# The last combination of a two-layer attention and mixture-of-experts kernel: eight buffer pairs, all loads at once, stores from ScalarE

## The chip, the cores and the metric

The kernel runs on one core of one Trainium2 chip. The metric is the device time of one execution in microseconds (us), as the median of several executions. Times inside the kernel come from the trace of one profiled execution and are counted from its first instruction.

## What is computed

The input `x` holds 8 sequences of 512 tokens with 128 features, float32. Four layers follow each other, each with a layer norm ahead of it and its result added to `x`:

```python
x = x + attn_a(layernorm(x), w_q, w_k, w_v1, w_v2)     # one head
x = x + ffn(layernorm(x), Wg, W1, W2, W3)              # 8 experts, each token goes to its best 2
x = x + attn_b(layernorm(x), Q, K, V, W)               # 16 heads
x = x + ffn(layernorm(x), Wg, W1, W2, W3)
return x
# in ffn:
topk_scores, topk_idx = top_k(xt @ Wg.T, 2)
y = einsum('teh,edh->ted', silu(xt @ W1) * (xt @ W2), W3)
out = sum over the token's two experts of topk_score * y[token, expert]
```

The change concerns the last line of the second `ffn`: for each token two rows of expert results are added to each other and to `x`, and the sum is the output.

## The kernel before

The kernel is a sequence of blocks: `prepare`, `attention_a`, `experts` ("f1"), `attention_b`, `experts` ("f2"). At the end of each block all engines meet: each one first drains itself, then signals, and nobody goes on before all have. These drains and signals are recorded with the line of the block's opening, L1032 for `experts`.

Within `experts`, 71 tiles of 128 rows (NT), already sorted by expert, pass through TensorE, ScalarE and VectorE. GpSimd (POOL) scatters each finished tile of results to the DRAM array `y_rows` with an indirect DMA (L1224): choice 0 of token n goes to row n, choice 1 to row 4096 + n. SyncE (SP) loads the tiles, and then waits until every scatter has landed (L1084).

Only in "f2" (`out` is not None) the final combination follows, sequence by sequence, b = 0 to 7 (NB), 256 KB per array and sequence:

- SP loads the two arrays of a sequence from `y_rows` into `yc[b % 2][0]` and `yc[b % 2][1]` (L1090). There are two such pairs, so that the load of sequence b waits until the additions of sequence b - 2 are done.
- POOL adds the pair (L1230).
- VectorE (DVE) adds the sum to the tokens in `x_tok` (L1214) and counts up `added`.
- SP stores the tokens of sequence b - 1 to the output (L1093, the last one L1096), in its program order behind the loads of sequence b and ahead of those of sequence b + 1, and waits at the end for all eight stores.

Both loads and stores move rows of 128 float32, 512 bytes each.

In "f1" there is no combination; it is done at the start of `attention_b`, which the change doesn't touch.

Of the kernel before, what the change touches and what calls it, by code (L numbers as in the profile page):

```python
# [4 lines left out]
F32 = mybir.dt.float32  # L5
F32R = mybir.dt.float32r
BF16 = mybir.dt.bfloat16
ALU = mybir.AluOpType
# [3 lines left out]
P = 128  # L12
NB, T, D = 8, 512, 128
QT = T // P
# [10 lines left out]
NK = 2  # L25
# [29 lines left out]
def wait(eng, sem, value):  # L55

    if not isinstance(value, int) or value > 0:
        eng.wait_ge(sem, value)
# [969 lines left out]
def experts(nc, g, name, pl, out=None):  # L1028
# [3 lines left out]
    with ExitStack() as ctx:  # L1032
        sb = lambda n, s, d: ctx.enter_context(nc.sbuf_tensor(f"{name}_{n}", s, d))
        pb = lambda n: ctx.enter_context(nc.psum_tensor(f"{name}_{n}", [P, 512], F32))
        sem = lambda n: ctx.enter_context(nc.semaphore(f"{name}_{n}"))
# [10 lines left out]
        y_sb = [sb(f"y_sb{i}", [P, D], F32) for i in range(NY)]  # L1046
        dest = sb("dest", [P, NT], I32)
        if out is not None:
            yc = [[sb(f"yc{i}_{k}", [P, QT, D], F32) for k in range(NK)] for i in range(2)]
        cleared = sem("cleared")  # L1050
        xs_in = [sem(f"xs_in{i}") for i in range(NX)]
        xs_turned = sem("xs_turned")
# [11 lines left out]
        y_done = sem("y_done")  # L1064
        y_out = [sem(f"y_out{i}") for i in range(NY)]
        if out is not None:
            yc_in = [sem(f"yc_in{i}") for i in range(2)]
            yc_summed = sem("yc_summed")
            added = sem("added")
            stored = sem("stored")  # L1070
        block = ctx.enter_context(nc.Block())

        @block.sync
        def _(sp):
            sp.wait_ge(pl.table_done, 2)
            for i in range(2):
                sp.wait_ge(pl.scattered[i], NB // 2 * NK * QT * 16)
            for i in range(NT):
                row = sp.value_load(pl.table[0:1, 1, i:i + 1], min_val=0, max_val=NE * CAP - P)
                wait(sp, hidden_done, i - NX + 1)  # L1080
                wait(sp, dest_done, i - NX + 1)
                sp.dma_start(xs[i % NX][:], g.x_sorted[bass.ds(row, P), :]).then_inc(xs_in[i % NX], 16)
            for i in range(NY):
                sp.wait_ge(y_out[i], len(range(i, NT, NY)) * 16)  # L1084
            if out is not None:
                for b in range(NB):
                    wait(sp, added, b - 1)
                    for k in range(NK):
                        rows = g.y_rows[k * CAP + b * T:k * CAP + b * T + T, :].rearrange("(t p) d -> p t d", p=P)
                        sp.dma_start(yc[b % 2][k][:], rows).then_inc(yc_in[b % 2], 16)  # L1090
                    if b > 0:
                        sp.wait_ge(added, b)
                        sp.dma_start(out[(b - 1) * T:b * T, :].rearrange("(t p) d -> p t d", p=P),  # L1093
                                     g.x_tok[:, (b - 1) * QT:b * QT, :]).then_inc(stored, 16)
                sp.wait_ge(added, NB)
                sp.dma_start(out[(NB - 1) * T:NB * T, :].rearrange("(t p) d -> p t d", p=P),  # L1096
                             g.x_tok[:, (NB - 1) * QT:NB * QT, :]).then_inc(stored, 16)
                sp.wait_ge(stored, NB * 16)

        @block.tensor  # L1100
# [60 lines left out]
        @block.scalar  # L1161
        def _(act):
            for s in range(NT + 2):
                if s < NT:
                    act.wait_ge(xs_turned, s + 1)
                    wait(act, up_full, s - 2)
                    nc.scalar.activation(xs_parts[s % 3][0][:], turn_bank[:, 0:P], ACT.Copy).then_inc(xs_hi_done, 1)
                i = s - 1
                if 0 <= i < NT:
                    act.wait_ge(gate_full, i + 1)  # L1170
                    wait(act, hidden_done, i - 1)
                    nc.scalar.activation(act_gate[i % 2][:], gate_bank[i % 2][:, 0:EH], ACT.Silu).then_inc(silu_done, 1)
                i = s - 2
                if 0 <= i < NT:
                    act.wait_ge(hid_turned, i + 1)
                    wait(act, y_full, i - 2)
                    nc.scalar.activation(hid_parts[i % 3][0][:], hid_bank[i % 2][:, 0:HW], ACT.Copy).then_inc(hid_hi_done, 1)  # L1177

        @block.vector
        def _(dve):  # L1180
            dve.wait_ge(pl.table_done, 2)
            dve.wait_ge(cleared, 4)
            for s in range(NT + 4):
                if s < NT:
                    dve.wait_ge(xs_in[s % NX], s // NX * 16 + 16)
                    nc.vector.copy_predicated(dest[:, s:s + 1], pl.valid[:, s:s + 1],
                                              xs[s % NX][:, DEST:DEST + 1].bitcast(I32)).then_inc(dest_done, 1)
                    dve.wait_ge(xs_hi_done, s + 1)
                    hi, lo = xs_parts[s % 3]
                    nc.vector.tensor_tensor(lo[:], turn_bank[:, 0:P], hi[:].bitcast(F32), ALU.subtract).then_inc(xs_lo_done, 1)  # L1190
                i = s - 1
                if 0 <= i < NT:
                    dve.wait_ge(up_full, i + 1)
                    dve.wait_ge(silu_done, i + 1)
                    wait(dve, hid_turned, i - 2)
                    nc.vector.scalar_tensor_tensor(hidden[i % 3][:, 0:EH], act_gate[i % 2][:], xs[i % NX][:, GATE:GATE + 1],
                                                   up_bank[i % 2][:, 0:EH], ALU.mult, ALU.mult).then_inc(hidden_done, 1)
                i = s - 4
                if 0 <= i < NT:
                    dve.wait_ge(y_full, i + 1)  # L1200
                    wait(dve, y_out[i % NY], i // NY * 16)
                    nc.vector.tensor_reduce(y_sb[i % NY][:], y_bank[:, 0:2 * P].rearrange("p (i d) -> p d i", i=2), AX.X,  # L1202
                                            ALU.add).then_inc(y_done, 1)
                i = s - 2
                if 0 <= i < NT:
                    dve.wait_ge(hid_hi_done, i + 1)
                    hi, lo = hid_parts[i % 3]
                    nc.vector.tensor_tensor(lo[:], hid_bank[i % 2][:, 0:HW], hi[:].bitcast(F32),  # L1208
                                            ALU.subtract).then_inc(hid_lo_done, 1)
            if out is not None:  # L1210
                for b in range(NB):
                    rows = g.x_tok[:, b * QT:b * QT + QT, :]
                    dve.wait_ge(yc_summed, b + 1)
                    nc.vector.tensor_tensor(rows, rows, yc[b % 2][0][:], ALU.add).then_inc(added, 1)  # L1214

        @block.gpsimd
        def _(pool):
            nc.gpsimd.memset(dest[:], NOWHERE).then_inc(cleared, 1)
            for h in hidden:
                nc.gpsimd.memset(h[:, EH:HW], 0.0).then_inc(cleared, 1)  # L1220
            for i in range(NT):
                pool.wait_ge(y_done, i + 1)
                pool.wait_ge(dest_done, i + 1)
                nc.gpsimd.indirect_dma_start(out=g.y_rows, out_offset=bass.IndirectOffsetOnAxis(dest[:, i:i + 1], 0),  # L1224
                                             in_=y_sb[i % NY][:], in_offset=None, bounds_check=NK * CAP - 1,
                                             oob_is_err=False).then_inc(y_out[i % NY], 16)
            if out is not None:
                for b in range(NB):
                    pool.wait_ge(yc_in[b % 2], (b // 2 + 1) * NK * 16)
                    nc.gpsimd.tensor_tensor(yc[b % 2][0][:], yc[b % 2][0][:], yc[b % 2][1][:],  # L1230
                                            ALU.add).then_inc(yc_summed, 1)


def attention_b(nc, g, pl):
# [370 lines left out]
def build(nc, ins, out):  # L1605
    g = Shared()
    g.spent = []
    with ExitStack() as ctx:
# [27 lines left out]
        with ExitStack() as half:  # L1636
            pl = Plan(nc, half, "f1_p")
            with ExitStack() as first:
                sb1 = lambda n, s: first.enter_context(nc.sbuf_tensor(n, s, F32R))
                pair1 = lambda n, s: (sb1(f"{n}_hi", s), sb1(f"{n}_lo", s))  # L1640
                g.xn_hi, g.xn_lo = pair1("xn", [P, NB * T])
                g.a_wq, g.a_wk = pair1("a_wq", [P, P]), pair1("a_wk", [P, P])
                g.a_wv1, g.a_wv2 = pair1("a_wv1", [P, KD]), pair1("a_wv2", [P, D])
                prepare(nc, g, ins)
                attention_a(nc, g, pl)
            experts(nc, g, "f1", pl)
        with ExitStack() as half:
            pl = Plan(nc, half, "f2_p")
            attention_b(nc, g, pl)
            experts(nc, g, "f2", pl, out)  # L1650
# [22 lines left out]
```

## Time and profile before

| | |
|---|---|
| median of three executions | 1532.55 us (1528.47 to 1534.16) |
| the profiled execution: time | 1528.65 us |
| its span, first to last instruction | 1526.9 us |
| part of the span from the first load of the combination | 1493.1 to 1526.9 us |
| POOL's last addition | 1519.6 to 1520.8 us |
| last store: issued, landed | 1521.6, 1523.9 us |
| last barrier signals | 1526.9 us |

The profile's page gives the span, the busy time of each engine, the share of each DMA engine's time that its packets took, and the chain of work that ended last. Views of the trace show single instructions in order of time, sums over a window, and the instructions of one line. "SPq" and "POOLq" are the instruction queues of the two engines; an entry there is an instruction that isn't counted as busy, such as a DMA issue or a drain.

### The profile page before, as it was taken

The numbers are of one execution on the slowest core, as the hardware profiler recorded it, in microseconds if no ns is written. First come the engines' busy times: TensorE is split into PE (matmuls) and PEld (weight loads), VectorE is DVE, ScalarE is ACT, GpSimd is POOL, SyncE is SP. The second block draws the span as 40 slices with busy tenths as digits, with TensorE's granted clock in tenths as the row PEclk, the third lists the DMA queues.
The fourth block names the chain that finished last, engine by engine and source line by source line (L and its number), as shares of the span: only waits on it lengthen the run. The fifth ranks groups of instructions, "written<-read, shape, count | busy, mean of one in ns | idle before, by whom it ended". The sixth has DMA issues, their size and how long they took to land. (4 is left out here: it accounts for less than half of the span.)

```text
span 1526.9 us, 28432 instructions
## 1 busy us (share of the span) xinstructions
PE 1309.5 (86%) x8377; PEld 1119.5 (73%) x8377; DVE 1098.0 (72%) x2822; ACT 941.9 (62%) x2522; POOL 765.3 (50%) x954
## 2 busy tenths in 40 slices
PE   1688635999679999999999999999999996399990
PEld 1576634999558888888888888888888885299980
DVE  5666544777548788888887888888888875277771
ACT  1554422444248888788788888787887884244440
POOL 3005563444335555575675665765765655244443
PEclk9986657999879999999999999999999997599995
DMA  9391011222100000000000000000000000122215
GB/s 180 115 378 37 29 38 50 62 61 60 38 28 1 2 15 1 1 25 5 5 25 1 20 10 1 22 8 2 11 5 5 10 3 11 34 62 59 60 45 165
DMA packets 91936, 64.47 MB, mean 42 GB/s; under 512 B 34020, under 2 KB 77935, under 8 KB 91792
## 3 DMA queue, kind: packets, MB, share of 16 engines
q1 hardware_dynamic: 83152, 45.75, 11.0%
q0 software_dynamic: 8640, 16.93, 3.5%
q8 instruction: 74, 1.21, 0.3%
q14 instruction: 70, 0.57, 0.1%
HBM read 26.59 MB, written 36.96 MB: 42 GB/s over the span
## 5 line engine op out<-in xcount | busy, mean ns | idle before, releaser
L1364 POOL TENSOR_TENSOR b_probs<-b_probs,b_recip 128x128 f32<-128x128 f32 (+3 forms) x512 | 352.7, 719 | 308.7 <-DVE b_recip L1597 308.7
L420 DVE TENSOR_TENSOR b_pt_lo<-b_ring,b_pt_hi 128x512 fp32r<-128x512 f32 (+1 forms) x384 | 219.0, 598 | 95.5 <-ACT b_pt_hi L414 90.1
L545 ACT ACTIVATE b_probs<-b_s_bank,b_neg_max 128x256 f32<-128x256 f32 (+3 forms) x512 | 267.9, 533 | 27.6 <-DVE b_neg_max L537 26.2
L537 DVE TENSOR_REDUCE b_neg_max<-b_s_bank 128x1 f32<-128x256 f32 (+3 forms) x512 | 219.7, 479 | 47.3 <-PE b_s_bank L529 46.3
L1224 POOL DMA_INDIRECT y_rows<-f_y_sb,f_dest x142 | 139.1, 979 | 193.4 <-DVE f_y_sb L1202 184.5
L414 ACT ACTIVATE b_pt_hi<-b_ring 128x512 fp32r<-128x512 f32 (+1 forms) x384 | 192.2, 547 | 11.4 <-PE b_ring L485 10.6
L485 PE MATMUL b_ring<-ident,b_probs 128*128 128x128 f32 x1280 | 179.1, 277 | 4.7 <-DVE b_q_lo L420 4.7
L81 PE MATMUL b_s_bank<-b_k_hi,b_q_hi 64*128 64x256 f32 (+3 forms) x512 | 180.6, 353 | 2.9 <-ACT b_probs L545 1.4
L1177 ACT ACTIVATE f_hid_hi<-f_hid_bank 128x384 fp32r<-128x384 f32 x142 | 69.9, 492 | 160.8 <-PE f_hid_bank L1130 143.7
L554 PE MATMUL b_pv_bank<-b_pt_hi,b_v 128*128 128x512 f32 (+3 forms) x512 | 160.0, 324 | 6.3 <-DVE b_y L1560 5.2
L82 PE MATMUL b_s_bank<-b_k_lo,b_q_hi 64*128 64x256 f32 (+3 forms) x512 | 164.4, 321 | 0.0
L83 PE MATMUL b_s_bank<-b_k_hi,b_q_lo 64*128 64x256 f32 (+3 forms) x512 | 163.8, 320 | 0.0
L485 PEld LDWEIGHTS b_ring<-ident,b_probs 128*128 128x128 f32 x1280 | 140.8, 141 | 21.6 <-DVE b_q_lo L420 10.8
L554 PE MATMUL b_pv_bank<-b_pt_lo,b_v 128*128 128x512 f32 (+3 forms) x512 | 148.1, 326 | 0.0
L1208 DVE TENSOR_TENSOR f_hid_lo<-f_hid_bank,f_hid_hi 128x384 fp32r<-128x384 f32 x142 | 79.2, 558 | 61.8 <-ACT f_hid_hi L1177 61.7
L1142 PE MATMUL f_y_bank<-w,f_hid_hi 128*128 x426 | 116.4, 342 | 3.5 <-DVE f_y_sb L1202 2.9
L81 PEld LDWEIGHTS b_s_bank<-b_k_hi,b_q_hi 64*128 64x128 f32 x512 | 95.2, 186 | 30.1 <-issue 15.0
L554 PEld LDWEIGHTS b_pv_bank<-b_pt_hi,b_v 128*128 128x128 f32 x512 | 97.7, 191 | 17.5 <-DVE b_pt_lo L420 6.2
L545 ACT ACTIVATION_READ_ACCUMULATOR b_probs<-b_s_bank,b_neg_max 128x1 f32 x512 | 108.4, 212 | 0.0
L554 PEld LDWEIGHTS b_pv_bank<-b_pt_lo,b_v 128*128 128x128 f32 x512 | 98.0, 191 | 8.4
L83 PEld LDWEIGHTS b_s_bank<-b_k_hi,b_q_lo 64*128 64x128 f32 x512 | 95.5, 187 | 6.1
L1142 PEld LDWEIGHTS f_y_bank<-w,f_hid_hi 128*128 128x128 f32 x426 | 79.9, 188 | 25.9 <-issue 21.9
(303 smaller groups left out, 3360.7 us busy)
## 6 DMA issues: line engine op xcount, KB each, us to landing
x_sorted<-a_blank SPq DMA_DIRECT2D x64, 260.0 KB, 3.8
f_xs<-x_sorted SPq DMA_DIRECT2D x142, 65.0 KB
b_yc<-y_rows SPq DMA_DIRECT2D x16, 256.0 KB, 3.1
f_yc<-y_rows SPq DMA_DIRECT2D x16, 256.0 KB, 3.3
y_rows<-f_y_sb,f_dest POOLq DMA_INDIRECT x142
x_tok<-in_L_attn_a_x_dram SPq DMA_DIRECT2D x8, 256.0 KB, 5.2
out_dram<-x_tok SPq DMA_DIRECT2D x8, 256.0 KB, 2.5
f_raw<-in_L_ffn_W_dram SPq DMA_DIRECT2D x1, 1408.0 KB, 6.4
```

The lines of the kernel that those rows point to most:

```text
L81: nc.tensor.matmul(out, st[0], mv[0], start=start, stop=False)
L82: nc.tensor.matmul(out, st[0], mv[1], start=False, stop=False)
L83: return nc.tensor.matmul(out, st[1], mv[0], start=False, stop=stop)
L414: nc.scalar.activation(dst, src(rg.of(key)), ACT.Copy).then_inc(rg.hi_done, 1)
L420: nc.vector.tensor_tensor(dst, src(rg.of(key)), hi.bitcast(F32), ALU.subtract).then_inc(rg.lo_done, 1)
L485: last = nc.tensor.transpose(rg.of(keys[k])[:, to:to + P], probs[:, P_AT[i] + j * P:P_AT[i] + j * P + P], ident[:])
L537: nc.vector.tensor_reduce(sc.neg_max[:, i:i + 1], s_tile(sc, i), AX.X, ALU.max, negate=True).then_inc(sc.max_done, 1)
L545: nc.scalar.activation(probs[:, P_AT[i]:P_AT[i] + (i + 1) * P], s_tile(sc, i), ACT.Exp, bias=sc.neg_max[:, i:i + 1], accum_out=sums[:, i:i ...
L554: last = nc.tensor.matmul(pv_bank[:, j * P:T], v_at(j), pt[part][:, PT_AT[j]:PT_AT[j] + T - j * P], start=(j == 0 and part == 0), stop=(j ...
L1142: nc.tensor.matmul(y_bank[:, 0:2 * P], hi[:, c * P:c * P + P], w3[:, bass.ds(at, 2 * P)], start=c == 0, stop=False)
L1224: nc.gpsimd.indirect_dma_start(out=g.y_rows, out_offset=bass.IndirectOffsetOnAxis(dest[:, i:i + 1], 0), in_=y_sb[i % NY][:], in_offset=Non ...
L1364: nc.gpsimd.tensor_tensor(part, part, recip[:, i:i + 1].to_broadcast([P, (i + 1) * P]), ALU.mult).then_inc(probs_done, 1)
```

## The change

Each of the eight sequences gets its own pair of buffers and its own semaphore. SP issues all sixteen loads with no wait between them. The stores are issued by ScalarE (ACT), each after `added` has reached its sequence. POOL does the first addition for even sequences only; for odd ones VectorE does it, counts `summing` up, waits for it and does the second addition.

```diff
         if out is not None:
-            yc = [[sb(f"yc{i}_{k}", [P, QT, D], F32) for k in range(NK)] for i in range(2)]
+            yc = [[sb(f"yc{b}_{k}", [P, QT, D], F32) for k in range(NK)] for b in range(NB)]
...
-            yc_in = [sem(f"yc_in{i}") for i in range(2)]
+            yc_in = [sem(f"yc_in{b}") for b in range(NB)]
             yc_summed = sem("yc_summed")
+            summing = sem("summing")
...
                 for b in range(NB):
-                    wait(sp, added, b - 1)
                     for k in range(NK):
                         rows = g.y_rows[k * CAP + b * T:k * CAP + b * T + T, :].rearrange("(t p) d -> p t d", p=P)
-                        sp.dma_start(yc[b % 2][k][:], rows).then_inc(yc_in[b % 2], 16)
-                    if b > 0:
-                        sp.wait_ge(added, b)
-                        sp.dma_start(out[(b - 1) * T:b * T, :].rearrange("(t p) d -> p t d", p=P),
-                                     g.x_tok[:, (b - 1) * QT:b * QT, :]).then_inc(stored, 16)
-                sp.wait_ge(added, NB)
-                sp.dma_start(out[(NB - 1) * T:NB * T, :].rearrange("(t p) d -> p t d", p=P),
-                             g.x_tok[:, (NB - 1) * QT:NB * QT, :]).then_inc(stored, 16)
+                        sp.dma_start(yc[b][k][:], rows).then_inc(yc_in[b], 16)
                 sp.wait_ge(stored, NB * 16)
...
         # ScalarE, after its last tile
+            if out is not None:
+                for b in range(NB):
+                    act.wait_ge(added, b + 1)
+                    act.dma_start(out[b * T:b * T + T, :].rearrange("(t p) d -> p t d", p=P),
+                                  g.x_tok[:, b * QT:b * QT + QT, :]).then_inc(stored, 16)
...
         # VectorE, after its last tile
                     rows = g.x_tok[:, b * QT:b * QT + QT, :]
-                    dve.wait_ge(yc_summed, b + 1)
-                    nc.vector.tensor_tensor(rows, rows, yc[b % 2][0][:], ALU.add).then_inc(added, 1)
+                    if b % 2:
+                        dve.wait_ge(yc_in[b], NK * 16)
+                        nc.vector.tensor_tensor(yc[b][0][:], yc[b][0][:], yc[b][1][:], ALU.add).then_inc(summing, 1)
+                        dve.wait_ge(summing, b // 2 + 1)
+                    else:
+                        dve.wait_ge(yc_summed, b // 2 + 1)
+                    nc.vector.tensor_tensor(rows, rows, yc[b][0][:], ALU.add).then_inc(added, 1)
...
         # GpSimd, after its last scatter
-                for b in range(NB):
-                    pool.wait_ge(yc_in[b % 2], (b // 2 + 1) * NK * 16)
-                    nc.gpsimd.tensor_tensor(yc[b % 2][0][:], yc[b % 2][0][:], yc[b % 2][1][:],
-                                            ALU.add).then_inc(yc_summed, 1)
+                for b in range(0, NB, 2):
+                    pool.wait_ge(yc_in[b], NK * 16)
+                    nc.gpsimd.tensor_tensor(yc[b][0][:], yc[b][0][:], yc[b][1][:], ALU.add).then_inc(yc_summed, 1)
```

## Rows read from the trace of the kernel before

**Rows 1.** Timeline, window 1484 to 1527: start us, duration us, engine, line, operation, [idle before <- releaser]

```profile
1490.87 0.98 POOL L1224 DMA_INDIRECT y_rows<-f_y_sb,f_dest  x1 [0.63 <-issue]
1493.12 2.03 SPq L1090 DMA_DIRECT2D f_yc<-y_rows  x4
1496.69 1.26 POOL L1230 TENSOR_TENSOR f_yc<-f_yc,f_yc 128x512 f32<-128x512 f32 x1 [4.85 <-DMA f_yc<-y_rows]
1497.98 0.69 DVE L1214 TENSOR_TENSOR x_tok<-x_tok,f_yc 128x512 f32<-128x512 f32 x1 [7.89 <-POOL f_yc L1230]
1498.68 1.26 POOL L1230 TENSOR_TENSOR f_yc<-f_yc,f_yc 128x512 f32<-128x512 f32 x1 [0.73 <-DMA f_yc<-y_rows]
1498.70 0.38 SPq L1093 DMA_DIRECT2D out_dram<-x_tok  x1
1499.13 1.09 SPq L1090 DMA_DIRECT2D f_yc<-y_rows  x2
1499.97 0.69 DVE L1214 TENSOR_TENSOR x_tok<-x_tok,f_yc 128x512 f32<-128x512 f32 x1 [1.30 <-POOL f_yc L1230]
...
1519.56 1.26 POOL L1230 TENSOR_TENSOR f_yc<-f_yc,f_yc 128x512 f32<-128x512 f32 x1 [2.44 <-DMA f_yc<-y_rows]
1520.86 0.69 DVE L1214 TENSOR_TENSOR x_tok<-x_tok,f_yc 128x512 f32<-128x512 f32 x1 [3.00 <-POOL f_yc L1230]
1521.58 0.38 SPq L1096 DMA_DIRECT2D out_dram<-x_tok  x1
```

**Rows 2.** Instructions of the block's line L1032: count, duration ns min/median/max, first and last start

```profile
L1032 POOLq EVENT_SEMAPHORE  x4: 17/17/17, 415.7 to 1526.8; - x4
L1032 POOLq DRAIN  x2: 7064/7115/7166, 408.6 to 1519.5; - x2
L1032 SPq COMPARE_BRANCH  x2: 33/37/41, 411.4 to 1523.9; - x2
L1032 SPq DRAIN  x2: 7/10/13, 411.5 to 1524.1; - x2
```

**Rows 3.** Waits of POOL at the start of "f1": waiting line <- releaser: us, times, longest

```profile
POOL f_dest L1218 <- POOLq L830: 5.5, 1, 5.5
```

**Rows 4.** Windows: length, engines' busy us (x instructions), PEclk, DMA busy share, GB/s

```profile
1494.00:1494.50 0.50, 0.00 (x0) 0.00 (x0) 0.00 (x0) 0.00 (x0) 0.00 (x0) 0.50 0.27 80
1494.50:1495.00 0.50, 0.00 (x0) 0.00 (x0) 0.00 (x0) 0.00 (x0) 0.00 (x0) 0.50 0.75 225
1495.00:1497.00 2.00, 0.00 (x0) 0.00 (x0) 0.00 (x0) 0.00 (x0) 0.31 (x1) 0.50 1.10 324
1498.50:1499.50 1.00, 0.00 (x0) 0.00 (x0) 0.18 (x1) 0.00 (x0) 0.82 (x1) 0.50 0.00 0
1499.50:1501.00 1.50, 0.00 (x0) 0.00 (x0) 0.69 (x1) 0.00 (x0) 0.44 (x1) 0.50 0.84 209
1506.00:1507.00 1.00, 0.00 (x0) 0.00 (x0) 0.00 (x0) 0.00 (x0) 0.79 (x1) 0.50 0.99 262
1509.50:1510.50 1.00, 0.00 (x0) 0.00 (x0) 0.00 (x0) 0.00 (x0) 1.00 (x1) 0.50 0.97 240
1513.00:1513.50 0.50, 0.00 (x0) 0.00 (x0) 0.00 (x0) 0.00 (x0) 0.50 (x1) 0.50 0.71 157
1499.50:1519.80 20.30, 0.00 (x0) 0.00 (x0) 4.15 (x6) 0.00 (x0) 6.99 (x7) 0.50 0.87 245
```

**Rows 5.** Stores of line L1093, issue to landing

```profile
L1093 SPq DMA_DIRECT2D out_dram<-x_tok x7: 377/378/378, 1498.7 to 1517.9; - x7
...
DMA to landing us min/median/max: 2.4/2.5/3.3
```

## The prediction

> **What bounds the kernel now.** The change touches nothing ahead of the first load of the combination, so I read the trace from its end, in four steps. First, the timeline of the last 35 us [rows 1]. The last scatter is issued at 1490.87, SP may load at 1493.12, and from there a cycle repeats: a pair of loads lands, POOL adds for 1.26 us, VectorE adds for 0.69, SP issues a store and then the next pair. The second of VectorE's additions starts at 1499.97, the eighth at 1520.86: six cycles of 3.48 us. TensorE and ScalarE do nothing.
>
> Second, what ends the kernel. The last store is issued at 1521.58, and SP is past its wait for it at 1523.9 [rows 1, 2]. But the span ends at 1526.9. The instructions of the block's line show why: POOL's drain starts at 1519.5 and takes 7.17 us, so until 1526.7; POOL's signals stand at 1526.8 [rows 2]. POOL's last addition ended at 1520.82 [rows 1], 5.88 us before the drain did. Is this cost tied to the stores? No: at the end of "f1", which stores nothing, the drain also takes 7.06 us [rows 2], and at the end of `attention_a`, without stores too, POOL's first instruction of "f1" waits 5.5 us for POOL's own drain [rows 3]. So POOL needs about 5.9 us after its last work, and it is not hidden. The end is (end of POOL's last addition) + 5.88 + 0.2. SP's side has 2.6 us of slack (1526.7 less 1524.1).
>
> Third, what POOL's last addition waits for: 2.44 us for the loads [rows 1]. Fourth, whether the loads can go faster: the windows [rows 4]. While only loads move, the core moves 324 GB/s. Between 1498.5 and 1499.5 nothing moves, as both buffer pairs are in use. From 1499.5 to 1519.8 the mean is 245 GB/s at a DMA share of 0.87. So this stretch is mostly bound by the transfers themselves and only by the missing 0.13 through waiting. That limits the change: all its waits together hide little DMA time.
>
> **The change, part by part.** *Loads at once.* Four loads take SP 2.03 us of issue [rows 1], 0.51 each; sixteen take about 8.6 us with the gaps, ahead of the transfers (0.26 MB at 324 GB/s is 0.81 us each). The loads start moving at 1494.0 as before. Until 1495 they move 0.15 MB (80 and 225 GB/s for half a microsecond each), then 324 GB/s [rows 4]. The first store is issued where it is now, at 1498.70: sequence 0 lands as before. Now that store's packets move from about 1499.6 (the window from 1499.5 is the first with traffic again [rows 4]); I take 1499.7. By then loads alone have moved 0.15 + 4.7 x 0.324 = 1.68 MB, where before 1.05 MB was all that was asked for.
>
> Let L7 be the time when the last pair has landed, L6 the one before. Until L7 move sixteen loads, 4.19 MB, and six stores (0 to 5), 1.57 MB: 5.77 MB, so 4.09 MB after 1499.7. At what rate? No row of before shows long mixed traffic. The nearest: windows in which a store and loads move with the engines nearly always busy, 262 and 240 GB/s [rows 4]; I take 250 for mixed traffic and 324 for loads alone. If a waiting store gets half of the engines, two thirds of the bytes move mixed: 1 / (0.67/250 + 0.33/324) = 271 GB/s. It is close to 245 / 0.87 = 282, the present mean without its idle share. Taken: 272. Then 4.09 MB last 15.0 us, L7 = 1514.7. A sequence (0.79 MB) takes 2.9 us instead of 3.48, L6 = 1511.8. Bounds: 209, the window in which the traffic turns from store to loads, and 324, the rate of loads alone [rows 4]. They give L7 = 1519.3 and L6 = 1515.5, or 1512.3 and 1509.9.
>
> *First additions split.* POOL's last addition is now that of sequence 6. Its chain: L6 + 0.07 (landing to start) + 1.26 + 5.88 + 0.2 = L6 + 7.4 = 1519.2. That it is not sequence 7 is worth the whole 2.9 us between L6 and L7. VectorE does sequence 7: 0.07 + 0.69 + 0.03 + 0.69 + 0.02 = 1.5 us until the store is issued, where POOL and VectorE took 2.02 (1519.56 to 1521.58). VectorE has 12 additions of 0.69, 8.3 us within some 18, POOL four of 1.26: neither becomes the bound.
>
> *Stores from ScalarE.* Eight issues of 0.38 us [rows 5] leave SP for an idle engine, and no load waits behind them; ScalarE has nothing behind them either. No row shows its price for an issue; I take SP's. If it were double, the store chain would be 0.4 us longer, and POOL's chain would still count almost alone. From the issue of the last store to SP's drain are 2.5 us (1521.58 to 1524.1), then 0.2 for the barrier: L7 + 1.5 + 2.5 + 0.2 = 1518.9. The two chains end together, POOL's just later.
>
> *Sum.* The end moves from 1526.9 to 1519.2: 7.7 us less. Of this 2.9 is POOL's release from the last sequence and 4.8 the denser transfers. The bounds give a gain of 4.0 us (209 GB/s: 1515.5 + 7.4 = 1522.9) and of 9.6 (324: 1517.3). The profiled execution took 1528.65 us with 1.75 outside its span; it would take 1520.95. It lies 3.9 us under the median of the runs, which becomes 1532.55 - 7.7 = 1524.8, or 0.50% less.
>
> The Trainium skill speaks against part of this ("DMA: Bandwidth & Descriptors", section "Issuing engines are not separate DMA queues"): DMAs from several engines run on the same sixteen DMA engines, and spreading them saves only issue time. The trace agrees that the engines are nearly full (0.87), and by this rule alone the stores on ScalarE would bring nothing; my sum credits them with nothing but the freedom of the loads.
>
> **The rivals.** *Loads first.* The sixteen loads are all queued before most stores are issued; stores could be served behind them. Then loads move at 324: 2.52 MB after 1499.7 last 7.8 us, L7 = 1507.5, POOL is done by 1513.3. The stores follow, 2.10 MB at about 250 GB/s or 8.4 us, plus 0.8 for the receipt and 0.4 for the barrier: 1517.1, 9.8 us less. For it: the loads' long lead, issued by about 1501.7. Against it: a store's packets moved promptly in [rows 4, 5] (2.5 us to landing, 3.3 at most) even with loads about. The same skill page (section "Queues, rings and completion order") says that ScalarE and SP own separate rings and each DMA engine takes them in turn, packet by packet. By this the stores aren't pushed back, and my sum holds; no row here shows two rings.
>
> *Mixing is dear.* If traffic in both directions all the time costs what the turn from one to the other costs now (209 GB/s), the gain is 4.0 us, no change that can be told. For it: every mixed window is slower than loads alone. Against it: 262 at a full share.
>
> *Slower.* If the alternation of the two rings held the rate at the 157 GB/s of the worst half microsecond [rows 4], 4.09 MB would last 26.1 us: L7 = 1525.8, end by the store chain 1530.0, 3.1 us more. The change loses as soon as L7 passes 1522.7 (1526.9 less 4.2), 23.0 us after 1499.7, which is a rate below 178 GB/s. Against it: that window has a share of only 0.71, so it also contains waiting, which more queued loads fill.
>
> *It does nothing*, if the DMA engines were full already: the share of 0.87 and the empty microsecond exclude this, and POOL's earlier release alone gives about 3 us.
>
> **How the numbers follow.** About 0.5% (7.7 us) is what a measurement of this kernel can tell from no change. Chances: the sum with its rates from 240 to 300 GB/s, 0.60, gains from 5 to 9 us and centred on 7.7, so half of it lies on each side of the limit; loads first or a rate above, 0.20, gain 9 to 10.5; mixing is dear, 0.16, gain 0 to 5; slower, 0.04, mostly by less than the limit. So faster 0.30 + 0.20 = 0.50, same 0.30 + 0.16 + 0.01 = 0.47, slower 0.03. The likeliest time is 1524.8. The range takes the first two cases and most of the third, with some 2 us of scatter of the runs: 1520.5 to 1529.5.
>
> **What would show it.** Right: sixteen load issues in a row until about 1502 without a wait; DMA share of 0.95 or more from 1495 to L7; POOL's last addition near 1512 and its drain some 7.1 us long, ending the kernel; stores landing within about 3 us. Wrong: stores that take 5 us or more to land (loads first), a rate below 240 GB/s at full share (mixing is dear), SP's wait for the stores ending after POOL's drain, or a drain that shrinks, which would break the main chain.

## The result and the profile after

| | before | changed |
|---|---|---|
| median of ten executions each | 1529.16 us (1524.49 to 1534.16) | 1518.39 us (1514.62 to 1522.70) |
| ratio | | 0.9934, interval 0.9921 to 0.9947 |
| profiled execution: time, span | 1528.65, 1526.9 us | 1514.62, 1512.6 us |
| first load of the combination to the end | 33.8 us | 24.7 us |

The kernel became faster by 0.66%, some 10.1 us (8.1 to 12.1); the two medians lie 10.8 us apart. The profiled executions lie 14 us apart; 5.2 us of that stand ahead of the first load (1493.1 against 1487.9), where the two kernels do the same. I therefore compare the stretch from the first load's issue (F) to the end: 9.1 us less.

The changed kernel's timeline from F; POOL's additions are L1233, VectorE's L1213 (first) and L1217 (second), the stores L1174:

```profile
1487.92 13.06 SPq L1090 DMA_DIRECT2D f_yc<-y_rows  x16
```

```profile
1491.60 1.26 POOL L1233 TENSOR_TENSOR f_yc<-f_yc,f_yc 128x512 f32<-128x512 f32 x1 [4.95 <-DMA f_yc<-y_rows]
1492.89 0.69 DVE L1217 TENSOR_TENSOR x_tok<-x_tok,f_yc 128x512 f32<-128x512 f32 x1 [8.00 <-POOL f_yc L1233]
1493.62 15.34 ACTq L1174 DMA_DIRECT2D out_dram<-x_tok  x8
...
1505.23 1.26 POOL L1233 TENSOR_TENSOR f_yc<-f_yc,f_yc 128x512 f32<-128x512 f32 x1 [4.10 <-DMA f_yc<-y_rows]
1506.53 0.69 DVE L1217 TENSOR_TENSOR x_tok<-x_tok,f_yc 128x512 f32<-128x512 f32 x1 [2.91 <-POOL f_yc L1233]
1507.14 0.68 DVE L1213 TENSOR_TENSOR f_yc<-f_yc,f_yc 128x512 f32<-128x512 f32 x1
1507.86 0.69 DVE L1217 TENSOR_TENSOR x_tok<-x_tok,f_yc 128x512 f32<-128x512 f32 x1
```

Against [rows 1]: the sixteen loads are issued in one go, and the last addition stands 20 us after F instead of 27.7. The issues take SP 13.1 us, where four took 2.03. POOL's last addition starts 17.3 us after F (1505.23), where it stood at 26.4. The block's own instructions, as in [rows 2]:

```profile
L1032 POOLq EVENT_SEMAPHORE  x4: 17/17/17, 414.0 to 1512.5; - x4
L1032 POOLq DRAIN  x2: 7066/7116/7166, 406.9 to 1505.2; - x2
L1032 SPq COMPARE_BRANCH  x2: 33/37/41, 409.6 to 1510.9; - x2
L1032 SPq DRAIN  x2: 7/10/13, 409.8 to 1511.1; - x2
```

POOL's drain still ends the kernel (1505.2 + 7.17 = 1512.4), 1.3 us behind SP. Windows of the changed kernel, as [rows 4]:

```profile
1489.00:1490.00 1.00, 0.00 (x0) 0.00 (x0) 0.00 (x0) 0.00 (x0) 0.00 (x0) 0.50 0.65 189
1490.00:1491.00 1.00, 0.00 (x0) 0.00 (x0) 0.00 (x0) 0.00 (x0) 0.00 (x0) 0.50 1.11 329
1491.00:1492.50 1.50, 0.00 (x0) 0.00 (x0) 0.00 (x0) 0.00 (x0) 0.90 (x1) 0.50 0.95 239
1494.50:1506.50 12.00, 0.00 (x0) 0.00 (x0) 4.92 (x8) 0.00 (x0) 3.79 (x3) 0.50 1.14 343
1506.50:1508.20 1.70, 0.00 (x0) 0.00 (x0) 1.64 (x3) 0.00 (x0) 0.00 (x0) 0.50 0.35 105
```

For 12 us, with loads and stores side by side, the core moves 343 GB/s at a share of 1.14. That is more than any window of before that I had taken for mixed traffic (240, 262), and it shows that a share of 1 was not full. (The share adds up the times of all packets; where packets of one engine overlap in time it comes out above 1.) Issue to landing of the stores, as [rows 5]:

```profile
L1174 ACTq DMA_DIRECT2D out_dram<-x_tok x8: 378/378/436, 1493.6 to 1508.6; - x8
...
DMA to landing us min/median/max: 2.3/5.3/6.5
```

The first store is issued 5.7 us after F (1493.62), about where it was before (5.6), but it doesn't move at once. The traffic by queue, from its issue to 1496.2 and then from F to the landing of the last pair but one (q1 holds SP's transfers, q10 ScalarE's):

```profile
q1 hardware_dynamic: 1725, 0.86, 110.7%
...
q1 hardware_dynamic: 8196, 4.07, 80.9%
q10 hardware_dynamic: 2126, 1.06, 20.4%
```

In the first of the two windows no packet of a store has moved yet, 2.6 us after the issue (2.1 in the second profile of the same kernel); the last store of before, with nothing beside it, was issued at 1521.58 and moved from 1522.5. Of the 1.57 MB of stores 0 to 5, 1.06 MB have moved when the last pair but one has landed.

### The profile page after: what moved, and what is told of

Read it like the earlier page. It is cut to its first block and busy times, and to the rows that moved or that the text cites. A ratio compares the mean times of both kernels' runs of the same rounds, so it can differ in the third digit from the quotient of the medians.

```text
span 1512.6 us, 28432 instructions
## 1 busy us (share of the span) xinstructions
PE 1302.4 (86%) x8377; PEld 1111.3 (73%) x8377; DVE 1100.1 (73%) x2826; ACT 941.5 (62%) x2522; POOL 760.4 (50%) x950
## 3 DMA queue, kind: packets, MB, share of 16 engines
q1 hardware_dynamic: 78928, 43.65, 10.8%
## 5 line engine op out<-in xcount | busy, mean ns | idle before, releaser
L545 ACT ACTIVATE b_probs<-b_s_bank,b_neg_max 128x256 f32<-128x256 f32 (+3 forms) x512 | 267.9, 533 | 27.7 <-DVE b_neg_max L537 26.3
```

Of the source, the lines that this page charges most:

```text
L545: nc.scalar.activation(probs[:, P_AT[i]:P_AT[i] + (i + 1) * P], s_tile(sc, i), ACT.Exp, bias=sc.neg_max[:, i:i + 1], accum_out=sums[:, i:i ...
```

## The experiments

The measure is the time from F to the end in one profiled execution. The changed kernel, profiled twice, gave 24.7 and 24.1; one variant gave 21.6 and 22.9. So differences under about 1.5 us are not told from scatter. The kernel before was profiled once, so that its 33.8 us carry such an error too. "The changed kernel" is the base of the diffs unless said otherwise.

### Stores back on SP, behind the loads

```diff
 # SP, after its sixteen loads (and no stores on ScalarE)
+                for b in range(NB):
+                    sp.wait_ge(added, b + 1)
+                    sp.dma_start(out[b * T:b * T + T, :]..., g.x_tok[:, b * QT:b * QT + QT, :]).then_inc(stored, 16)
```

> The stores go back to SP, behind all sixteen loads; the rest is the changed kernel. Measure: the time from the first load's issue (F) to the end, 33.8 us before, 24.7 us in the changed kernel. Theory 'depth' (343 GB/s came because many transfers were queued, whoever issues them): loads alone keep 343, the last pair lands near F + 14, the stores of 2.1 MB follow at about 343 too, end near F + 21.5 to 22.5. Rival 'second ring' (343 with both directions needs ScalarE's own queue): in the stretch where stores run, the rate falls to 250 or less, end at F + 24 or later.

Measured: 21.6 us. Two windows, the first from 5.0 us after F, the second behind the landing of the last load (VectorE starts to add that pair at 1509.23):

```profile
1498.40:1509.00 10.60, 0.00 (x0) 0.00 (x0) 6.31 (x10) 0.00 (x0) 4.18 (x3) 0.50 1.15 345
1509.40:1512.40 3.00, 0.00 (x0) 0.00 (x0) 1.21 (x2) 0.00 (x0) 0.00 (x0) 0.50 1.14 343
```

One queue keeps 345 GB/s as well as two do, so ScalarE's queue is not what raised the rate. The run was even shorter than the changed kernel: SP's loads go first, and the stores fill the end without the pause of 1506.5 to 1508.2. The end is now set by the stores (SP's drain at 1514.8), 0.4 us behind POOL's.

The same kernel, profiled again and timed:

> The kernel of e1_stores_on_sp, timed. Its time from the first load to the end repeats within 0.5 us of 21.6; against the kernel before 33.8 - 21.6 = 12.2 us or a ratio of 0.992; 3 us under the changed kernel, at the edge of what five rounds can tell. Rival (the 3 us were an accident of one execution): the same ratio as e14 and a time from the first load of 24 or more.

22.9 us, ratio 0.9926 (0.9897 to 0.9954). The changed kernel beside it:

> The changed kernel unchanged, for a second profile and a second timing on the chip on which e15 is timed. The time from the first load to the end repeats within 0.5 us of 24.7; ratio to before 0.992 to 0.995.

24.1 us, ratio 0.9953 (0.9930 to 0.9976). In the stretch the order "loads first" wins 1.2 to 3.1 us; in the whole time the intervals overlap, so there the gain is not shown.

### All first additions on GpSimd, or none

```diff
-                for b in range(0, NB, 2):      # GpSimd; VectorE without the branch for odd b
+                for b in range(NB):
```

> GpSimd does all eight first additions again, the rest is the changed kernel. If GpSimd's drain ends the kernel, the end is (last pair landed) + 0.07 + 1.26 + 5.88 + 0.2; in the changed kernel the last pair landed about 1.9 us after the last but one, so F to end is 26.6 instead of 24.7 us. Rival (the last store ends it, the drain is covered): 0.5 us more for the slower first addition, 25.2.

26.2 us, 1.5 to 2.1 more. The drain's row, the signals' and SP's:

```profile
L1032 POOLq EVENT_SEMAPHORE  x4: 17/17/17, 414.8 to 1515.5; - x4
L1032 POOLq DRAIN  x2: 7064/7115/7166, 407.7 to 1508.2; - x2
L1032 SPq DRAIN  x2: 7/10/13, 410.6 to 1512.8; - x2
```

SP is through at 1512.8, POOL's drain only at 1515.4. The opposite edit removes GpSimd's loop and lets VectorE add all:

```diff
+                    dve.wait_ge(yc_in[b], NK * 16)
+                    nc.vector.tensor_tensor(yc[b][0][:], yc[b][0][:], yc[b][1][:], ALU.add).then_inc(summing, 1)
+                    dve.wait_ge(summing, b + 1)
```

> VectorE does all eight first additions, GpSimd none. If the drain is a cost behind GpSimd's last work, it now runs from the last scatter on and is over long before the stores, which set the end: last store landed 23.0 us after F plus 0.4, so 23.4 to 23.6 instead of 24.7. Rival (the drain's 5.9 us are the kernel's end whatever GpSimd did last, or VectorE with 16 additions of 0.69 becomes the bound): 24.7 or more.

23.2 us, 0.9 to 1.5 less, which the time alone would not tell from scatter; the rows do. Now the drain is covered:

```profile
L1032 POOLq DRAIN  x2: 7052/7058/7064, 408.9 to 1489.0; - x2
L1032 SPq DRAIN  x2: 7/10/13, 411.8 to 1514.5; - x2
```

It starts behind the last scatter (1489.0) and is over at 1496; the span ends at 1514.7, with SP. So the 5.9 us are a cost behind GpSimd's last work, whatever that is, and can be hidden. All these drains end blocks in which GpSimd had issued indirect DMAs. In the one block of the kernel before without them, `prepare`, the drain takes 0.4 us, beside GpSimd's last work:

```profile
L175 POOLq DRAIN  x1: 406/406/406, 53.7 to 53.7; - x1
```

That the indirect DMAs are what the long drain waits for is likely by this, but no run changes them alone. The same edit in the kernel before, with its two pairs and SP's stores:

> The kernel before, with one part of the change carried to its end: VectorE does all first additions, GpSimd none; two pairs and stores on SP stay. GpSimd's drain is then covered, the end is the last store (2.6 us less), and each sequence is added in 1.4 us instead of 1.95, which brings its store 0.5 us earlier: F to end 33.8 - 2.6 - 8 x 0.3 to 0.5 = 27 to 29 us. Rival (the loads, not the additions, set the cycle of 3.48 us): 33.8 - 2.6 - 0.5 = 30.7.

28.2 us, 5.6 less than before: the largest step of any single edit to the kernel before. 2.6 us of it are the covered drain. Each sequence also leaves its buffers sooner: VectorE's second addition to the tokens starts at 1497.70 and its eighth at 1515.62, a cycle of 2.99 us instead of 3.48, which is 2.9 us over six cycles. The transfers are the same, so they had not set the cycle.

### How many pairs

```diff
-            yc = [[...] for b in range(NB)]                  # 8 pairs
+            yc = [[...] for b in range(2)] * (NB // 2)       # 2 pairs; with 4: range(4), NB // 4
...
                 for b in range(NB):
+                    wait(sp, added, b - 1)                   # with 4: b - 3
```

> The changed kernel with two pairs of buffers instead of eight: SP waits for the additions of two sequences earlier before it loads; stores on ScalarE and the split additions stay. Theory 'depth': the rate falls back to about 245 to 280 GB/s and windows with DMA idle return; the cycle is some 3.0 us (0.5 less than before, as loads no longer stand behind stores on SP and odd sequences are added in 1.4 us instead of 1.95): F to end 29 to 31. Rival 'second ring': near 343 GB/s also with two pairs, F to end 25 to 26.

31.2 us. Two neighbouring windows and the whole stretch:

```profile
1498.90:1502.90 4.00, 0.00 (x0) 0.00 (x0) 0.26 (x1) 0.00 (x0) 1.26 (x1) 0.50 1.14 343
1502.90:1504.90 2.00, 0.00 (x0) 0.00 (x0) 1.71 (x3) 0.00 (x0) 0.00 (x0) 0.50 0.10 26
1492.00:1518.00 26.00, 0.00 (x0) 0.00 (x0) 7.68 (x12) 0.00 (x0) 5.04 (x4) 0.50 0.76 225
```

With two pairs the traffic runs at full rate too, but stops while both pairs are held by landing, additions and the next issue. The total lies just above the 29 to 31 us expected. The idle windows came as expected, the rate of 245 to 280 GB/s did not: 343 in the bursts, 225 in the mean.

> The changed kernel with four pairs of buffers. Theory 'depth': what counts is that the DMA queues don't run empty; six to eight transfers in flight (some 1.5 to 2 MB, 5 us of work) cover the 5 us from a load's issue to its addition, so F to end is within 1 us of 24.7. If all sixteen loads must be ahead of the stores: 27 or more.

23.5 us: four pairs do what eight do, within the scatter. So of the change's three parts, each measured by taking it back alone, the deeper queue is worth the most, 6.5 to 7.1 us (31.2 without it), the split additions 1.5 to 2.1 (26.2), and the stores on ScalarE nothing (21.6 and 22.9 with them on SP).

### ScalarE's stores alone, in the kernel before

```diff
 # kernel before: SP's stores removed, ScalarE's loop of the change added
```

> The kernel before with one part of the change alone: ScalarE issues the stores; two pairs and all first additions on GpSimd stay. By the prediction this part brings only the freedom of the loads: a load issue stands 0.42 us earlier in each cycle, F to end 33.8 - 8 x 0.4 = 31 at the least, 33.8 at the most; end set by GpSimd's drain. Rival (a second queue lets both directions run at once at full rate): 29 or less.

33.1 us, 0.7 less, which is within the scatter. Here too bursts and pauses:

```profile
1493.60:1496.60 3.00, 0.00 (x0) 0.00 (x0) 0.00 (x0) 0.00 (x0) 0.88 (x1) 0.50 1.13 339
1496.60:1498.60 2.00, 0.00 (x0) 0.00 (x0) 0.69 (x1) 0.00 (x0) 1.01 (x2) 0.50 0.46 138
```

The bytes now move at 339 GB/s while they move, and the total hardly changes: with two pairs the rate in the bursts doesn't set the time.

### Are the stores what slows the stretch?

The kernel before without its first seven stores:

```diff
                     if b > 0:
                         sp.wait_ge(added, b)
-                        sp.dma_start(out[(b - 1) * T:b * T, :]..., g.x_tok[:, (b - 1) * QT:b * QT, :]).then_inc(stored, 16)
```

> The kernel before without its first seven stores (the waits ahead of them stay; these rows of the output are not written). If waits bound the two-pair kernel, only seven issues of 0.42 us go: first load to end 33.8 - 2.9 = 31. If the mixed traffic bound it at about 250 GB/s, 1.84 MB less saves 7 us: 26.5 to 27.5.

30.0 us, 3.8 less, of which 2.9 are SP's seven issues of 0.42 each. Nearly a third of the bytes went, and the mean rate of the stretch fell with them:

```profile
1490.50:1511.00 20.50, 0.00 (x0) 0.00 (x0) 4.21 (x7) 0.00 (x0) 8.81 (x7) 0.50 0.68 201
```

So the kernel before was mostly bound by its waits, not by its traffic: by the round of issue, landing, additions and next issue that each pair goes through. The changed kernel without the stores of sequences 0 to 5 (`for b in range(6, NB)` in ScalarE's loop):

> The changed kernel without the stores of sequences 0 to 5 (these rows of the output are not written). Loads alone at 343 GB/s: the last pair lands at about F + 14 instead of F + 19.1, the last but one at F + 12.5, GpSimd's drain ends F + 20: 20 to 20.5 instead of 24.7, and what the stores cost the loads is 4.5 us. If stores ran beside loads free of charge: 24 or more.

21.3 us; POOL's last addition started 13.7 us after F (1502.0 less 1488.3) instead of 17.3. The stores that run beside the loads delay the last addition by 3.6 us. The 1.06 MB of them that had moved by then would last 3.1 us alone at 343 GB/s: the loads lose about what the stores' bytes take. The end was later than expected by 1 us, as the early dip cost more and POOL's last addition lasted 1.54 us.

### Directions apart

```diff
 # ScalarE (or, in the second run, SP), ahead of its stores
+                        for c in range(NB):
+                            act.wait_ge(yc_in[c], NK * 16)
```

> The changed kernel, but ScalarE issues no store before all loads have landed, so that the two directions hardly mix. If mixed traffic cost anything, separating it would win: loads at 343 GB/s alone land by F + 14, stores of 2.1 MB at 343 last 6.1 us, end of the last store near F + 21.5, and GpSimd's chain ends near F + 20: 21.9 instead of 24.7. If stores alone are slower (281 GB/s in the last store of before), 23.2. If separating gains nothing: 24.7 or more.

24.9 us. Separating gains nothing, and the stores alone were slower, 287 GB/s:

```profile
1512.00:1517.00 5.00, 0.00 (x0) 0.00 (x0) 0.35 (x1) 0.00 (x0) 0.00 (x0) 0.50 1.02 287
```

> e5_stores_held with the held stores issued by SP instead of ScalarE. In e5 the stores alone moved at 287 GB/s with packets of 27 to 45 ns, in the end of e1 at 343 with packets of 27 ns. If the queue makes that difference (ScalarE's stores are slower than SP's), here the stores run at 343 and F to end is 23.7 instead of 24.9. If it comes from stores with no load beside or ahead of them, 287 again and 24.9.

24.4 us and again 287 GB/s (window of 4 us), so this rate isn't ScalarE's queue. In the first experiment the stores behind the last load moved at 343 from the same SP queue. What makes the difference, perhaps that the queue had not run empty, is open.

### A version without first additions

VectorE adds both arrays straight to the tokens, each as it lands; the last sequence is finished and stored in halves; GpSimd does nothing.

```diff
+                    dve.wait_ge(yc_in[b][0], 16)
+                    nc.vector.tensor_tensor(rows, rows, yc[b][0][:], ALU.add).then_inc(summing, 1)
+                    dve.wait_ge(summing, b + 1)
+                    dve.wait_ge(yc_in[b][1], 16)
+                    n = QT // 2 if b == NB - 1 else QT
+                    for t in range(0, QT, n):
+                        part = g.x_tok[:, b * QT + t:b * QT + t + n, :]
+                        nc.vector.tensor_tensor(part, part, yc[b][1][:, t:t + n, :], ALU.add).then_inc(added, 1)
```

> A version meant to beat both: no first additions, VectorE adds both arrays straight to the tokens as each lands, the last sequence is finished and stored in two halves, GpSimd does nothing. The end is the store chain; after the last load come 0.07 + 0.36 + 0.38 + some 2.2 us, 1.3 less than with two full additions, and no drain behind: F to end 22.0 to 22.6 against 24.7. Against the kernel before 11 to 12 us less, a ratio of about 0.9925 on the base of the changed kernel's 0.9934. Rival (16 waits on single loads slow VectorE): 24 or more.

22.7 us, ratio 0.9928 (0.9909 to 0.9947). With its stores issued by SP behind the loads:

> e7_direct with its nine stores issued by SP behind the sixteen loads, as in e1_stores_on_sp. In e1 the DMA engines never paused until the last store, and F to end was 21.6 us; e7 had pauses behind F + 18 and 22.7. If the order (loads first, stores filling the end) is what counts and the additions are no longer on the path, this has 21.2 to 21.6 and a ratio near 0.992. Rival (the last sequence's additions still set the end in e1): 20.5 or less. Rival (SP's issue, 0.7 us each under back-pressure, is the bound): above 21.6.

21.3 us, the shortest of those that write the whole output; ratio 0.9933 (0.9908 to 0.9958). The whole time does not tell these versions from the changed kernel.

## Why the prediction was off

**The time** came out at 1518.39, under the range's 1520.5. The forecast of 1524.8 was 6.4 us too high. By its parts: the base was the median of three executions, 1532.55; over ten it is 1529.16, 3.4 us lower, and the absolute forecast carries this. The rest, 3.1 us, is gain: the medians lie 10.8 us apart (10.1 by the ratio, 8.1 to 12.1), forecast were 7.7. The range left 4.3 us below the forecast, so either error alone would have stayed within it. As a ratio the forecast was 0.9950, just outside the interval of the first measurement and inside that of the second (0.9930 to 0.9976).

**The step that failed** in the sum is the rate of mixed traffic, taken as 272 GB/s. Measured were 343. I read the windows with 240 and 262 GB/s as "engines nearly always busy" because their share was 0.97 and 0.99, and divided 245 by 0.87 for the rate at a full share. But [rows 4] itself has a window at a share of 1.10 and 324 GB/s: full is about 1.14, and 0.87 is only 0.76 of full. The kernel before shows the full share and the pause side by side:

```profile
1508.00:1508.50 0.50, 0.00 (x0) 0.00 (x0) 0.20 (x1) 0.00 (x0) 0.00 (x0) 0.50 1.14 343
1508.50:1509.00 0.50, 0.00 (x0) 0.00 (x0) 0.00 (x0) 0.00 (x0) 0.00 (x0) 0.50 0.47 138
```

The share explains most of the low mean, not all. Per unit of share the mean of before carried 282 GB/s (245 / 0.87), the changed kernel 301 (343 / 1.14), and the two windows that I took only 247 and 265: there the packets also lasted longer. Why they did is open; it isn't that loads and stores mix, since they mix at 343 in the changed kernel. From this misreading followed the reading that the stretch was "mostly bound by the transfers themselves". Three runs showed that it was mostly bound by waits: leaving out seven stores saved 3.8 us instead of some 7, freeing GpSimd shortened the cycle to 2.99 us with the same transfers, and with ScalarE's stores alone the bytes moved at 339 without a gain. With 343 GB/s the prediction's own sum gives L7 = 1511.6, L6 = 1509.3 and an end at 1516.7, a gain of 10.2 us against 9.1 to 9.7 in the stretch.

**What made up for part of it:** the start. I had 1.68 MB moved by 6.6 us after F; it was 1.48 MB (227 GB/s from 1488.0 to 1494.5). The windows of the changed kernel show a dip to 239 GB/s from 3.1 to 4.6 us after F, ahead of any store. The other profiles with queued loads have it at the same place, with 208 to 294 GB/s in their slowest microsecond there. So has the kernel before with GpSimd freed, at two pairs (229), so the depth alone doesn't make it. In sum L6 came 17.2 us after F (1505.16, 0.07 ahead of POOL's addition) and L7 at most 19.2, where I had 18.7 and 21.6 (1511.8 and 1514.7 less 1493.1).

The sixteen issues took SP 13.1 us instead of the 8.6 that I had from four. They still ran ahead of the transfers, and no run shows that this cost time.

**The chain at the end was right.** POOL's drain ends the kernel, 7.17 us long, 7.4 us behind L6: 17.2 + 7.4 = 24.6, measured 24.7. The share of it that I gave to POOL's release from the last sequence, 2.9 us, was too large, since the last two sequences now follow each other in some 2 us: giving POOL all additions cost 1.5 to 2.1.

**Stores on ScalarE** were credited with nothing of their own. That was right: in the kernel before they bring 0.7 us, within the scatter, and in the changed kernel they are no gain: issued by SP behind the loads, the stretch is 1.2 to 3.1 us shorter. The Trainium skill's rule ("DMA: Bandwidth & Descriptors", section "Issuing engines are not separate DMA queues"), that spreading the issue saves only sequencer time, agrees with both.

**Half the engines for a waiting store** was not what came: the first store moved nothing for 2.1 to 2.6 us, where I had 1.0, stores took 5.3 us to land (median) instead of 2.5, and of the bytes up to L6 a fifth were stores'. **Loads first**, a rival with 0.20, was in part the case: stores start late and land past its sign of 5 us. But they didn't stay behind the loads (1.06 MB had moved by L6), and L7 came up to 19.2 us after F, not 14.4. The variant on SP does put the loads first. Its 9.8 us gain is close to the measured one for another reason, and its 0.8 us for the receipt was too much: the last store of before had moved by 1523.5, and SP went on at 1523.9. **Mixing is dear** and **slower** are refuted by 343 GB/s in mixed traffic.

**What remains open:** the early dip, the late start of the first store, the longer packets in some windows of before, the 287 GB/s of stores alone, and 1 us between the stretch's 9.1 to 9.7 and the whole time's 10.1, which lies within its interval.

## What to carry to other kernels

Before calling a stretch bound by DMA, look for the highest share that the trace shows anywhere, and measure every other window against that, not against 1; then ask by an experiment whether fewer bytes or fewer waits make it shorter. When engines meet at the end of a block, see which one's drain ends last and let the engine with the dear one finish early; here taking the additions off GpSimd was worth 5.6 us in the kernel before by itself. Queue depth pays until the pauses are gone, four pairs here, and it costs nothing to put stores behind the loads on the same queue.

## What the runs showed of the hardware

- GpSimd's drain at the end of a block lasted until 5.9 us after its last work in the two `experts` blocks (5.3 at the end of `attention_a`, where the last scatter ended at 237.9 and the drain at 243.3), also when that work was an ordinary addition 29 us after the last indirect DMA. In the block without indirect DMAs it took 0.4 us. It can run beside other engines' work.
- Deep queues of 512-byte rows moved 343 to 345 GB/s over 7 to 12 us: loads alone (344, changed kernel without six stores), mixed with stores from two queues (343) or from one (345). SP's issue then waits: up to 2.16 us for one, 13.1 us for sixteen.
- Behind deep loads on SP's queue, the first store issued by ScalarE moved nothing for 2.1 to 2.6 us; the last store of before, with nothing beside it, moved after 0.9 us.
- GpSimd's addition of 1.26 us took up to 1.54 us where VectorE's additions ran beside it. From the changed kernel without six of its stores:

```profile
L1233 POOL TENSOR_TENSOR f_yc<-f_yc,f_yc x4: 1256/1336/1536, 1491.9 to 1502.0; 128x512 f32<-128x512 f32 x4
```
